# Row tiles loaded in float32 from two queues, and the gate chain moved ahead of the row statistics, in a fused attention-plus-FFN layer

## The reference

```
xn  = layernorm(x)                            # per row, no weights
q, kv = xn @ W_q.T, xn @ W_kv.T               # 16 heads of 128
qf, kvf = fft(q), fft(kv), each divided by its norm over the head
vh  = ifft(qf * cumsum(kvf, over the rows)).real
x1  = x + layernorm(vh @ W_o.T)
l3  = layernorm(x1)
logits = l3 @ gate_w.T + gate_b               # 8 experts
top two logits, softmax over them             # weights W8, 8 per row, 6 of them 0
xA  = l3 @ lora_A  (8 experts x rank 16)
ffn = l3 @ W.T + b + (xA * W8) @ lora_B
out = x1 + layernorm(ffn)
```

## Time and profile before

| | us |
|---|---|
| median of 3 runs | 1708.27 (1704.5 to 1710.08) |
| the profiled execution | 1708.1 |
| its span, slowest core (core 1) | 1706.6 |
| spans of the 8 cores | 1696.0 to 1706.6 |
| block ph1: until its last copy ends | 83.15 |
| block d: from its first load to the end | 1232.8 to 1706.6 |

### The profile page before, as it was taken

The page is one execution under the profiler, slowest core; times in us unless marked ns, Lnnn a source line. Parts: engine busy times, 40 slices in busy tenths (PEclk is TensorE's granted clock), DMA queues, the critical chain, the costliest instruction groups (busy, mean ns, idle before and its releaser), DMA issues. The chain is left out here.

```text
span 1706.6 us, 15368 instructions; the slowest of 8 cores (1696.0 to 1706.6 us)
## 1 busy us (share of the span) xinstructions
PE 1292.0 (76%) x5664; PEld 536.7 (31%) x5664; DVE 697.5 (41%) x977; ACT 445.4 (26%) x442; POOL 95.6 (6%) x186
## 2 busy tenths in 40 slices
PE   3479999979999946556665379999567777778774
PEld 2334444424444411111111034444233333333332
DVE  3500000000000048999999614444334445444544
ACT  3410110111011136666666300000022323132322
POOL 1100000000000021000000101111100000000000
PEclk9999999989999976666666589999779787878787
DMA  6522221122122129992000164444302121212121
GB/s 103 99 39 36 37 36 26 25 37 34 29 37 38 25 27 111 111 111 37 1 1 0 33 203 123 122 112 111 104 33 74 38 75 37 75 37 74 38 75 50
DMA packets 22801, 102.98 MB, mean 60 GB/s; under 512 B 3376, under 2 KB 3512, under 8 KB 20168
## 3 DMA queue, kind: packets, MB, share of 16 engines
q0 software_dynamic: 22112, 101.76, 29.1%
q1 hardware_dynamic: 616, 0.23, 0.1%
HBM read 128.24 MB, written 41.94 MB: 100 GB/s over the span
## 5 line engine op out<-in xcount | busy, mean ns | idle before, releaser
L310 PE MATMUL PMAIN<-AR,OV 128*128 128x512 bf16 x2048 | 458.1, 382 | 38.2 <-ACT AR L336 13.6
L310 PEld LDWEIGHTS PMAIN<-AR,OV 128*128 128x128 bf16 x2048 | 197.3, 98 | 299.4 <-issue 75.6
L349 DVE TENSOR_TENSOR OV<-AR 128x2048 bf16<-128x2048 bf16 x32 | 39.2, 1226 | 492.3 <-ACT AR L339 492.3
L856 PE MATMUL PAUX<-AR 128*128 128x512 bf16 x1024 | 234.1, 391 | 0.0
L431 ACT ACTIVATE AR<-PAUX 128x1024 bf16<-128x1024 f32 x128 | 124.0, 1021 | 75.0 <-DVE AR L511 42.6
L856 PEld LDWEIGHTS PAUX<-AR 128*128 128x128 bf16 x1024 | 101.3, 100 | 126.6 <-issue 13.9
L336 ACT ACTIVATE AR<-PMAIN 128x1024 bf16<-128x1024 f32 x32 | 32.8, 1024 | 414.7 <-PE PMAIN L310 414.6
L585 PE MATMUL PMAIN<-AR 128*128 128x512 bf16 x512 | 116.2, 388 | 19.9 <-DMA AR<-wotb_s 19.9
L585 PE MATMUL PAUX<-AR 128*128 128x512 bf16 x512 | 111.8, 379 | 0.0
L478 PE MATMUL PAUX<-AR,MSIN 128*128 128x512 bf16 x128 | 56.4, 562 | 54.5 <-ACT AR L431 54.5
L753 DVE BATCH_NORM_STATS2 STAT<-AR 128x6 f32<-128x512 bf16 x64 | 39.5, 681 | 117.6 <-DMA AR<-x1s 117.6
(11 more groups left out here) (117 smaller groups left out, 1199.5 us busy)
## 6 DMA issues: line engine op xcount, KB each, us to landing
AR<-x POOLq DMA_DIRECT2D x32, 512.0 KB, 5.4
out<-AR POOLq DMA_DIRECT2D x16, 1024.0 KB, 5.1
OV<-wqs POOLq DMA_DIRECT2D x16, 512.0 KB, 5.2
OV<-wkvs POOLq DMA_DIRECT2D x16, 512.0 KB, 5.1
wotb_s<-wot POOLq DMA_DIRECT2D x16, 512.0 KB, 40.4
wtb_s<-wt POOLq DMA_DIRECT2D x16, 512.0 KB, 109.0
AR<-wotb_s POOLq DMA_DIRECT2D x16, 512.0 KB, 14.4
x1s<-AR POOLq DMA_DIRECT2D x16, 512.0 KB, 2.9
```

The source lines that it names most:

```text
L310: ins = te.matmul(PMAIN[:, nn * 512:(nn + 1) * 512], lhsT, XCT[:, c * 2048 + nn * 512: c * 2048 + (nn + 1) * 512], start=(c == 0), stop=(c ...
L349: v.tensor_mul(SQ[h % 2], DEST[:, h * 2048:(h + 1) * 2048], DEST[:, h * 2048:(h + 1) * 2048]).then_inc(s_sq, 1)
L856: te.matmul(PAUX[:, nn * 512:(nn + 1) * 512], lhsT, WTB[:, c * 2048 + nn * 512: c * 2048 + (nn + 1) * 512], start=(c == 0), stop=False)
```

## The change

There are two edits. In ph1, the buffers XRL become float32 and move from AR3 to AR1 (which is free there), so the load of x converts nothing and lands twice the bytes; and the odd tiles are issued by SP, the even ones by POOL. In d, `gates_head(t-1)` goes ahead of the wait for tile t of x1 and its statistics on DVE, and on ACT the sigmoid for tile t-1 goes ahead of the square root for tile t.

```
-    XRL = [AR3[:, 0:2048], AR3[:, 2048:4096]]
+    AR1_F = AR1.bitcast(F32)
+    XRL = [AR1_F[:, 0:2048], AR1_F[:, 2048:4096]]
...
             sy.dma_start(SEL4[:, :], sel4_d.ap()).then_inc(s_const, 16)
+            for t in range(1, NT, 2):
+                if t >= 2:
+                    sy.wait_ge(s_m, t - 1)
+                sy.dma_start(XRL[1], x_d.ap()[t * 128:(t + 1) * 128, :]
+                             ).then_inc(s_xp[1], 16)
...
-            for t in range(NT):
+            for t in range(0, NT, 2):
                 if t >= 2:
                     g.wait_ge(s_m, t - 1)
-                g.dma_start(XRL[t % 2], x_d.ap()[t * 128:(t + 1) * 128, :]
-                            ).then_inc(s_xp[t % 2], 16)
+                g.dma_start(XRL[0], x_d.ap()[t * 128:(t + 1) * 128, :]
+                            ).then_inc(s_xp[0], 16)
...
             for t in range(NT):
+                if t >= 1:
+                    gates_head(v, t - 1)
                 v.wait_ge(s_x1rp[t % 2], 16 * (t // 2 + 1))
...
                 v.bn_aggr(AGGR, STAT[:, :]).then_inc(s_st3, 1)
-                if t >= 1:
-                    gates_head(v, t - 1)
                 v.wait_ge(s_sq3, t + 1)
...
         def _(a):
             for t in range(NT):
-                a.wait_ge(s_st3, t + 1)
-                a.activation(COLS[:, 0:1], AGGR4[:, 1:2], AF.Sqrt,
-                             bias=EPSC).then_inc(s_sq3, 1)
                 if t >= 1:
                     tt = t - 1
                     a.wait_ge(s_gate1, tt + 1)
                     a.wait_ge(s_xas, tt)
                     a.activation(COLS[:, 3:4], COLS[:, 7:8], AF.Sigmoid
                                  ).then_inc(s_gate2, 1)
+                a.wait_ge(s_st3, t + 1)
+                a.activation(COLS[:, 0:1], AGGR4[:, 1:2], AF.Sqrt,
+                             bias=EPSC).then_inc(s_sq3, 1)
```

## The result

| | us |
|---|---|
| kernel before, median of 8 runs | 1707.32 |
| kernel after, median of 8 runs | 1657.27 (1655.49 to 1658.96) |
| ratio after to before | 0.9708, 95% interval 0.9697 to 0.9719 |
| predicted | 1648, range 1636 to 1666 |

The kernel is 50 us faster, and 9 us slower than forecast. In some executions of any kernel a part of the cores runs at a lower clock and takes longer: such runs are left out of the ratios and of the times of the experiments, and because cores 6 and 7 lost some 20 us in this way between ph1 and d in the profiled execution after (1676 us), block d is read on core 0 (span 1651.8) and stages by the median of the eight cores.

The account below looks back on a forecast made before the run. Taken as the bound: block d's cycle, where PE waits for DVE's gate chain and DVE for the x1 load. 1708.1 - 56 (new order) - 3.5 (clock) + 1 (behind last C) - 2 (ph1) = 1648 us, range 1636 to 1666.

Parts of the forecast that it names:

- Step 1: Block d, DVE: the gate chain of 4.6 us leaves the path and fits whole into DVE's idle 7.2 us.
- Step 2: Block d: statistics to F (start of L764) take 4.82 us instead of 7.41, a gain of 2.6.
- Step 3: Block d: one table load before L744 goes; L744 ends 1.28 us earlier, at 6.94 after C (end of L773).
- The landing: Block d: the load of x1 still lands 5.96 us after issue, so statistics start at 14.0 after C.
- Step 4: Block d: PE idles less, so its clock drops less often; half of the 14 cycles gain 0.48 us, 3.5 taken.
- ph1: Float32 loads of x from two queues: a gain of 2 us, between 0 and 4.4.
- (A): Block d: the x1 tile doesn't land earlier, so the gain is 38 us and the time 1666; chance 0.10.
- (B): Block d: PE becomes the bound, its bias matmuls ending at 20.0 after C; time 1668; chance 0.08.
- (C): ph1: float32 loads take time by landed bytes, 31 us more; time 1681; chance 0.04.
- (D): ph1: the two-queue float32 loads back up, 66 us more; time 1716, slower than before; chance 0.01.
- (E): Whole kernel: the edits do next to nothing, since PE's wait is not for the gate chain; time 1705; chance 0.01.
- the way behind the last C: End of the kernel: PE may no longer be at 2.4 GHz there, 1 us lost.

Follow-up runs that it names:

- e5: Both edits, plus a one-column sigmoid on ACT behind each copy L810, which forces the second table load back in; 1677.74 us, ratio 0.9820 to the kernel before.
- e7: Kernel before with the new order in d alone, the square root's table loaded early and POOL's load ahead of its store; 1601.71 us, ratio 0.9373.
- e4: Both edits, but all 16 float32 loads of x in ph1 issued by POOL alone; 1655.28 us, ratio 0.9688 to the kernel before.
- e3: Both edits, plus a one-column square root on ACT behind each sigmoid, loading its table early; 1640.45 us, ratio 0.9596 to the kernel before.
- e6: Both edits, with POOL in block d issuing the next tile's load ahead of the store; 1625.32 us, ratio 0.9512 to the kernel before.
- e2: Kernel before with only the ph1 edit, float32 loads of x from two queues; 1710.35 us, ratio 1.0015 to the kernel before.
- e1: Kernel before with only the new order in block d; 1654.45 us, ratio 0.9677 to the kernel before.

## Why the prediction was right, and where it was 9 us off

- **Step 1, the gate chain leaves the path: right.** It runs from 6.9 to 11.5 after C, for the 4.6 us read from the earlier trace rows, and DVE still waits 2.6 us behind it.
- **Step 2, from the statistics to F: right.** 1415.20 - 1410.31 = 4.89 against 4.82 from the earlier trace rows.
- **Step 3, one table load less in front of the result: right.** L750 ends at 6.94, as worked out; e5 puts the load back and gets 8.2, and 14 cycles that are 20 us longer.
- **The landing.** 6.0 to 6.3 us from the issue instead of 5.96, so F came at 19.1 in the mean and not at 18.9. The gain from C to F was 3.9 per cycle and not 4.0: about 1.5 us in all.
- **Step 4, the clock: the right direction and too much of it.** I counted 3.5 us; F to C fell by 0.07 us per cycle, 1 us. The mechanism had a hole. L874 ran at 2.4 GHz in the timeline above (1.02 us for what took 1.86), but PE then waited 1.2 us more for the normalisation, and L841 and L855 ran at 1.2 GHz all the same (1.01 and 1.97 us, against 0.61 and 1.11 in e7). I had looked at the gap before L874 alone (1.3 us here), and there is a second one of 1.2 us right behind it. That the two together let the clock fall is my reading. For it: in the three of the 14 cycles of core 0 in which L874 waited 0.48 us only, the transposes behind it ran at 2.4 GHz with both edits already:

```profile
1464.97 1.02 PE L874 MATMUL PAUX<-OV,AR 128*128 128x512 bf16 x4 [0.48 <-DVE AR L728]
...
1466.89 0.61 PE L841 MATMUL PMAIN<-IDENT,AR 128*128 128x128 bf16 x8 [0.90 <-ACT AR L802]
```

  In e7, with the first gap at 0.5 us and the second at 0.1 to 0.8, the clock fell once in 14 cycles of core 1. The half that I took of the cycles was thus three in 14.
- **ph1: the sign was wrong.** I took a gain of 2, between 0 and 4.4, and the loads cost 2, by the last copy. The steady part moved within 1 us, as the rows of equal rate had said; what I left out is that a second queue has its transfer under way beside the first one from the start, so the first tile, for which everybody waits, comes 1.7 us later. I had written that POOL's even loads no longer stand behind odd ones, and did not ask what stands beside them. The 1.2 us per load for the added bytes, an estimate from the price that the Trainium skill gives (page "DMA: Bandwidth & Descriptors", section "Anatomy of one DMA"), has the right sign for another reason: e4, with the same bytes in one queue, has a stage of 83.1 us, 1 longer than before and not 9. The landing of 5.4 us that I read for the loads of x was no figure of ph1, as said above, so I set the sign of being wrong, loads later than 6 us, where the loads before nearly were; SP's did pass it, with 6.1 to 6.2 us on most cores. ACT's waits for loads, another of my signs, could tell nothing: before, they already differ from 6 to 28 us between the cores.
- **Rivals.** (A) fell: the load was issued 1.28 us earlier and landed 1.2 earlier. (B) fell: on cores 0 to 3 L867 ended at 16.3 to 19.2 and never at 20, and e3 and e6 took F down to 17.9 and 17.0 and the cycle followed each time. The 0.4 us between the two chains that I read from one old cycle were no limit, since PE's end at 18.4 was itself late only because PE had begun at 1.2 GHz after its long wait; it moves to 16.3 when the wait goes. (C) and (D) fell with e2, which is 2 to 3 us slower than before and not 30 or more; (E) fell with e1, where the order alone takes some 54 us off.

The sum, term by term: 2.5 us of the 9 are the clock, about 1.5 the landing, 4 ph1, and 0.5 the way behind the last C, where I put 1 us and it is 1.5. About half a us is left, within what the medians of such runs differ by. All of these went the same way, and the time lies outside the 1640 to 1655 that I called my own range. It lies inside the stated 1636 to 1666 because that was drawn wide enough for (A), and (A) is not what happened; for that part the range was right by luck, while the 55 us of the new order were right by their working.

## What to carry to other kernels

When work is moved off a path, read what it had been hiding: here the gate chain had covered a table load, which a one-column activation placed in an idle moment takes off the path again, for 17 us. In one DMA queue, issue first what the next step waits for; putting a load ahead of a store that the same event releases was worth more than half of the whole change. And a second queue was no second path here: it made the one transfer that everybody waited for later.

## What the runs showed of the hardware that I had not expected

- A 512 KB load issued 0.5 us behind a 1 MB store on the same queue lands after 6.0 us, ahead of it after 4.4; the store pays 1.2.
- A first load that reads 1 MB lands at 10.0 us alone, at 10.4 with one more and at 10.2 with three more behind it in its queue (the last with conversion to bf16), and at 12.0 to 13.0 with one beside it in another queue.
- PE's clock follows the waits of others: over like stretches of block d the granted clock was 0.82 in the kernel before, 0.87 with both edits and 0.99 in e7, and the end of PE's matmuls moved from 17.6 to 19.3 after C in nine of 14 cycles to 16.3 in 13 of 14. Taking a wait away thus paid twice.
